# Masking and merging the live columns of the second query tile's two key tiles in a fused attention and expert kernel

## The reference

```python
xn = _layernorm(x)                       # (32, 256, 128)
Q, K, V = heads of xn @ Wq + bq, xn @ Wk, xn @ Wv
R = heads of xn @ Wr + br                # 10 position weights per head and row
d = jnp.arange(t)[:, None] - jnp.arange(t)[None, :]
valid = (d >= 0) & (d < maxlen)          # maxlen = 128
bias = jnp.where(valid, 0.0, NEG)
D_ntT = jnp.where(valid[None], b_nd[:, jnp.clip(d, 0, maxlen - 1)], 0.0)
extra = jnp.einsum('bhtn,ntp->bhtp', R, D_ntT)
logits = jnp.einsum('bhtd,bhpd->bhtp', Q, K) / math.sqrt(dq) + bias + extra
A = softmax(logits) @ V
out = x + (A joined) @ Wproj + bproj + experts(xn)
```

## Time and profile before

| | us |
|---|---|
| three timed runs | 1551.13, 1552.23, 1553.66 |
| median | 1552.23 |
| the profiled execution | 1553.0 |
| its span, first to last instruction | 1551.2 |
| TensorE busy | 1447.6 |
| VectorE busy | 1000.2 |
| ScalarE busy | 941.6 |
| GpSimd busy | 809.5 |
| transposes L1381, 1536 | 256.2 busy |
| copies L1073, 512 | 280.5 busy |
| sums L1093, 1024 | 304.7 busy |

### The profile page before, as it was taken

The page is one execution under the profiler, slowest core; times in us unless marked ns, Lnnn a source line. Parts: engine busy times, 40 slices in busy tenths (PEclk is TensorE's granted clock), DMA queues, the critical chain, the costliest instruction groups (busy, mean ns, idle before and its releaser), DMA issues.

```text
span 1551.2 us, 42996 instructions
## 1 busy us (share of the span) xinstructions
PE 1447.6 (93%) x11335; PEld 1157.8 (75%) x11335; DVE 1000.2 (64%) x3715; ACT 941.6 (61%) x2864; POOL 809.5 (52%) x1515
## 2 busy tenths in 40 slices
PE   2473999999999999999999999899999999999997
PEld 1132777777777777778999999677777777777776
DVE  4677777777777777772112211587778887877776
ACT  1130776767767676775455444477667677776765
POOL 0341777667776677671000000377766667777765
PEclk7695999999999999999999999899999999999999
DMA  9865765565666665545666665666665656666652
GB/s 284 279 237 178 211 184 163 169 176 171 180 174 181 170 177 170 166 138 170 207 200 202 203 211 181 175 180 174 180 177 169 176 164 180 175 181 177 176 166 66
DMA packets 375832, 283.10 MB, mean 183 GB/s; under 512 B 16635, under 2 KB 349989, under 8 KB 375717
## 3 DMA queue, kind: packets, MB, share of 16 engines
q1 hardware_dynamic: 367524, 265.16, 58.1%
q0 software_dynamic: 8192, 16.79, 3.4%
HBM read 168.57 MB, written 113.26 MB: 182 GB/s over the span
## 4 chain that ended last, share of the span: by engine, by line
PE 86%; SPq 5%; DVE 4%; issue 2%; ACT 1%; DMA 1%; POOL 0%; DVEq 0%; ACTq 0%; POOLq 0%
PE ps L1392 13%; PE ps L1412 12%; PE ps L1381 11%; PE ps L1281 9%; PE ps L1317 9%; PE ps L1282 9%; PE ps L1283 9%; PE ps L1422 9%; PE ps L1352 4%; SPq L435 1%; PE ps L1299 1%; SPq L396 1%; SPq L416 1%; DMA xn_d<-xn 1%; SPq L450 1%
## 5 line engine op out<-in xcount | busy, mean ns | idle before, releaser
L792 ACT ACTIVATE prob<-logit,low 128x128 f32<-128x128 f32 (+1 forms) x1024 | 454.4, 445 | 269.2 <-DVE low L1093 236.1
L1093 DVE CUSTOM_DVE_ANT_0 logit<-ps,extra 128x128 f32<-128x128 f32 (+1 forms) x1024 | 304.7, 353 | 155.9 <-issue 125.3
L1073 DVE COPY probT<-ps 128x384 f32<-128x384 f32 x512 | 280.5, 550 | 76.8 <-PE ps L1381 64.3
L666 POOL TENSOR_SCALAR prob<-prob,inv 128x128 f32<-128x128 f32 x512 | 190.5, 372 | 230.9 <-DVE inv L1083 220.4
L1381 PE MATMUL ps<-ident,prob 128*128 128x128 f32 x1536 | 256.2, 277 | 0.1
L668 POOL TENSOR_SCALAR prob<-prob,inv 128x256 f32<-128x256 f32 x512 | 243.2, 475 | 0.0
L1392 PE MATMUL ps<-qk 64*128 64x128 f32 (+1 forms) x2048 | 238.5, 351 | 0.7 <-DVE low L1093 0.7
L1381 PEld LDWEIGHTS ps<-ident,prob 128*128 128x128 f32 x1536 | 184.4, 141 | 40.2 <-issue 17.8
L1412 PE MATMUL ps<-probT,val 128*64 128x256 f32 (+1 forms) x2048 | 194.7, 332 | 4.3 <-DVE probT L1073 4.2
L641 POOL CAST r_hi<-r_raw 120x512 fp32r<-120x512 f32 x64 | 39.7, 620 | 297.3 <-ACT r_raw L763 297.2
L792 ACT ACTIVATION_READ_ACCUMULATOR prob<-logit,low 128x1 f32 x1024 | 191.7, 187 | 0.0
(11 more groups left out here) (171 smaller groups left out, 2544.6 us busy)
## 6 DMA issues: line engine op xcount, KB each, us to landing
skew<-gst SPq DMA_DIRECT2D x256, 256.0 KB
extra<-skew SPq DMA_DIRECT2D x128, 512.0 KB, 3.9
extra<-skew SPq DMA_DIRECT2D x128, 256.0 KB, 2.9
w1b<-w_d SPq DMA_DIRECT2D x39, 514.0 KB, 3.5
w2b<-w_d SPq DMA_DIRECT2D x39, 320.0 KB, 3.3
x_place<-zero SPq DMA_DIRECT2D x39, 256.0 KB, 2.8
placed<-x_place SPq DMA_DIRECT2D x39, 256.0 KB, 3.7
y_place<-yrow SPq DMA_DIRECT2D x39, 256.0 KB, 2.2
```

The costliest lines, as they stand in the source:

```text
L666: nc.gpsimd.tensor_scalar(prob[:, h, 0:P], prob[:, h, 0:P], inv[:, h, 0:1], 1.0, ALU.mult, ALU.mult).then_inc(norm_made, 1)
L792: ins = nc.scalar.activation(prob[:, h % PB, a:b], logit[:, h % LB, a:b], ACT.Exp, scale=-1.0, bias=low[:, h % LB, t:t + 1], accum_out=tot ...
L1073: nc.vector.tensor_copy(probT[:, h % 4, :], ps[:, PT_BANK[h % 2], 0:3 * P]).then_inc(pT_made, 1)
L1093: ins = nc.vector.tensor_tensor_reduce(out=logit[:, h % LB, a:b], in0=ps[:, S_BANK[n], a:b], in1=extra[:, h, a:b], scale=1.0, scalar=BIG, ...
```

## The change

The second query tile's logits are merged before the sums: a predicated copy on VectorE writes, for both heads at once, the logits of key tile 1 over those of key tile 0 where c <= p (`upto`). From there on a head has 2 x 128 columns instead of 3 x 128: `extra`, `logit`, `prob` shrink, the second sum, exponent and norm product have 128 columns, and two blocks are transposed. As the merged block holds weights for both key tiles, `copy_probs` writes it twice into `probT`, multiplied by 0/1 masks (`keep`), so that the value matmuls stay as they were. The position term has no fill in the second tile: each unit of it is written twice side by side (columns 0:128 and 128:256 of the scratch row) and the shifted read of 128 columns wraps round. The fill of the second tile's scratch falls away. The wide logits are issued before the narrow ones. GpSimd makes the masks at the beginning.

```diff
@@ memory
-        extra = sb("extra", [P, H, 3 * P])
+        extra = sb("extra", [P, H, 2 * P])
-        logit = sb("logit", [P, LB, 3 * P])
+        logit = sb("logit", [P, LB, 2 * P])
-        prob = sb("prob", [P, PB, 3 * P])
+        prob = sb("prob", [P, PB, 2 * P])
+        upto = sb("upto", [P, P])
+        keep = sb("keep", [P, 3 * P])
@@ SP
-            for tile in range(2):
-                sp.dma_start(skew_rows(tile, 0, H, P, P, ROW),
-                             fill[:, :].unsqueeze(1).broadcast_to([P, H, P])).then_inc(filled, 16)
+            sp.dma_start(skew_rows(0, 0, H, P, P, ROW),
+                         fill[:, :].unsqueeze(1).broadcast_to([P, H, P])).then_inc(filled, 16)
...
-                sp.dma_start(skew_rows(t, PER * g, PER, 0, P, ROW),
-                             gst[:, t, :].rearrange("p (h j) -> p h j", h=PER)
-                             ).then_inc(skew_out[t], 16)
+                src = gst[:, t, :].rearrange("p (h j) -> p h j", h=PER)
+                sp.dma_start(skew_rows(t, PER * g, PER, 0, P, ROW), src).then_inc(skew_out[t], 16)
+                if t == 1:
+                    sp.dma_start(skew_rows(t, PER * g, PER, P, P, ROW), src).then_inc(skew_out[t], 16)
...
-                wait_apart(sp, skew_out[t], (i * GROUPS + g + 1) * 16, filled)
+                wait_apart(sp, skew_out[t], (i * GROUPS + g + 1) * 16 * (t + 1), filled)
...
-                if t == 0:
-                    dst, src = extra[:, PER * g:PER * g + PER, 0:P], skew_rows(0, PER * g, PER, P - 1, P, ROW - 1)
-                else:
-                    dst, src = extra[:, PER * g:PER * g + PER, P:3 * P], skew_rows(1, PER * g, PER, -1, 2 * P, ROW - 1)
+                dst, src = extra[:, PER * g:PER * g + PER, t * P:(t + 1) * P], skew_rows(t, PER * g, PER, P - 1, P, ROW - 1)
@@ GpSimd: upto = 1 where c <= p; keep = 1 | p > c | c >= p
+            nc.gpsimd.memset(upto[:, :], 1.0).then_inc(mask_made, 1)
+            nc.gpsimd.memset(keep[:, :], 1.0).then_inc(mask_made, 1)
...
@@ ScalarE
-                        for t, (a, b) in enumerate(((0, P), (P, 3 * P))):
+                        for t, (a, b) in enumerate(((0, P), (P, 2 * P))):
@@ VectorE
-                wait_from(dve, skew_out[t], (seq * GROUPS + g) * 16)
+                wait_from(dve, skew_out[t], (seq * GROUPS + g) * 16 * (t + 1))
...
-                nc.vector.tensor_copy(probT[:, h % 4, :], ps[:, PT_BANK[h % 2], 0:3 * P]).then_inc(pT_made, 1)
+                nc.vector.tensor_tensor(probT[:, h % 4, 0:2 * P], ps[:, PT_BANK[h % 2], 0:2 * P], keep[:, 0:2 * P], ALU.mult)
+                nc.vector.tensor_tensor(probT[:, h % 4, 2 * P:], ps[:, PT_BANK[h % 2], P:2 * P], keep[:, 2 * P:],
+                                        ALU.mult).then_inc(pT_made, 1)
...
-                        for t, (a, b) in enumerate(((0, P), (P, 3 * P))):
+                        for t, (a, b) in enumerate(((0, P), (P, 2 * P))):
+                            if t == 1:
+                                nc.vector.copy_predicated(ps[:, 0:2, P:2 * P], upto[:, :].bitcast(U32).unsqueeze(1).broadcast_to([P, 2, P]),
+                                                          ps[:, 0:2, 2 * P:3 * P]).then_inc(logit_merged, 1)
+                                wait_apart(dve, logit_merged, i * PAIRS + j + 1, const_made)
@@ TensorE
-                for n in range(3):
+                for n in range(2):
                     mm = nc.tensor.transpose(ps[:, PT_BANK[h % 2], n * P:(n + 1) * P],
...
-                for q, k, cols in ((slice(0, P), slice(0, P), slice(0, P)), (slice(P, T), slice(0, T), slice(P, 3 * P))):
+                for q, k, cols in ((slice(P, T), slice(0, T), slice(P, 3 * P)), (slice(0, P), slice(0, P), slice(0, P))):
```

More of the change, by code:

```diff
@@ L211, in build @@
         assert top[0] <= yrow_at + 4 * 3 * P * 4
-        assert shared + (2 * ROW1 + 2 * ROW2 + ROWS_AHEAD * PER * E) * 4 <= shared + H * 3 * P * 4
+        assert shared + (2 * ROW1 + 2 * ROW2 + ROWS_AHEAD * PER * E) * 4 <= position_end
         top[0] = max(attention_end, prep_end)
@@ L298, in build @@
         s_psum = sem("s_psum")
+        logit_merged = sem("logit_merged")
         logit0_made = sem("logit0_made")
@@ L502, in spread_body @@
                 positions(i + 1, POSITIONS_AHEAD)
-            sp.wait_ge(filled, 32)
+            sp.wait_ge(filled, 16)
             for u in range(2):
@@ L607, in _ @@
             nc.gpsimd.memset(ones[:, :], 1.0).then_inc(const_made, 1)
+            nc.gpsimd.memset(upto[:, :], 1.0).then_inc(mask_made, 1)
+            nc.gpsimd.memset(keep[:, :], 1.0).then_inc(mask_made, 1)
+            pool.wait_ge(mask_made, 5)
+            nc.gpsimd.affine_select(out=upto[:, :], in_=upto[:, :], compare_op=ALU.is_ge, fill=0.0, base=0,
+                                    pattern=[[-1, P]], channel_multiplier=1).then_inc(mask_made, 1)
+            nc.gpsimd.affine_select(out=keep[:, P:2 * P], in_=keep[:, P:2 * P], compare_op=ALU.is_gt, fill=0.0, base=0,
+                                    pattern=[[-1, P]], channel_multiplier=1).then_inc(mask_made, 1)
+            nc.gpsimd.affine_select(out=keep[:, 2 * P:], in_=keep[:, 2 * P:], compare_op=ALU.is_ge, fill=0.0, base=0,
+                                    pattern=[[1, P]], channel_multiplier=-1).then_inc(mask_made, 1)
             pool.wait_ge(centred, 3)
@@ L1008, in _ @@
                 src, d = dst, 2 * d
-            upto = src
-            nc.vector.tensor_copy(tally[:, :], upto[:, TILES - 1, :]).then_inc(tally_made, 1)
+            upto_all = src
+            nc.vector.tensor_copy(tally[:, :], upto_all[:, TILES - 1, :]).then_inc(tally_made, 1)
             dve.wait_ge(counts_psum, 1)
@@ L1036, in _ @@
                                                 in1=counts[:, 0, :], op0=ALU.mult, op1=ALU.add))
-            link(nc.vector.tensor_tensor(upto[:, :, :], upto[:, :, :], chosen[:, :, :], ALU.subtract))
-            link(nc.vector.tensor_tensor(upto[:, :, :], upto[:, :, :], first[:, :].unsqueeze(1).broadcast_to(wide),
+            link(nc.vector.tensor_tensor(upto_all[:, :, :], upto_all[:, :, :], chosen[:, :, :], ALU.subtract))
+            link(nc.vector.tensor_tensor(upto_all[:, :, :], upto_all[:, :, :], first[:, :].unsqueeze(1).broadcast_to(wide),
                                          ALU.add))
             for k, one in enumerate((one1, one2)):
-                link(nc.vector.tensor_tensor(lg2[:, :, :], one[:, :, :], upto[:, :, :], ALU.mult))
+                link(nc.vector.tensor_tensor(lg2[:, :, :], one[:, :, :], upto_all[:, :, :], ALU.mult))
                 link(nc.vector.tensor_reduce(r1[:, :], lg2[:, :, :], AX_X, ALU.add))
@@ L1065, in weights @@
                                                in1=r_raw[:, k, :], op0=ALU.mult, op1=ALU.add).then_inc(r_made, 1)
-            dve.wait_ge(mask_made, 2)
+            dve.wait_ge(mask_made, 8)
             def copy_probs(i, h):
```

5 lines of the change are left out of this document (3 added, 2 removed).

## The result

The changed kernel takes 1545.3 us (median of six, 1542.8 to 1547.3), the kernel before 1552.3 beside it: a ratio of 0.9945, 95% interval 0.9934 to 0.9956. The forecast was 1524.4 us. The sign is right, and 7 us came where 28 were expected. The profiled execution took 1542.8 us, its span is 1541.0. Lines of the changed kernel: logits L1408 (before L1392), values L1428 (L1412), transposes L1397 (L1381), merge L1104, sums L1109 (L1093), masked products L1083 and L1084 (the copy L1073), `rT` L1074 (L1064), rounding on GpSimd L651, `low` and `logit` are written by the sums.

What follows compares the result with a forecast made beforehand. TensorE, busy 93% of the span, was taken as the bound, with VectorE next to be late. Terms -55.8 + 6.6 + 21.9 + 3 - 3.5 = -27.8 us took the median 1552.2 to 1524.4 us; range 1500 to 1562.

Steps and rivals of the forecast that it cites:

- Transposes, -55.8 us: TensorE: one of three transposes per head goes, 512 in all at 0.109 us; sequences 32.9 instead of 34.6 us.
- Order of the logits, 0: TensorE: issuing wide logits first is worth 0, bounds -0.05 to +0.05 us a pair.
- VectorE's prices: VectorE per pair: narrower sums -0.24, merge with wait +0.52, masked products +0.18; together +0.46 us.
- my case: Main forecast: merge row 0.42 us, partial stalls of TensorE, 1510 to 1535 us; chance 0.44.
- rival B: VectorE's merge reads two PSUM streams one after the other, row 0.69 us: 1544 us in all; chance 0.20.
- rival C: VectorE becomes the bound, merge passing source, old destination and mask singly, row over 0.9 us: 1565 us; chance 0.17.
- First half, slot 5 to 6, 0.41 us: TensorE waits for VectorE's second probability copy: 0.41 us per sequence, 16 x 0.41 = 6.6 us.
- the second half, slots 4 to 6, 1.37 us: TensorE stalls behind VectorE, 0.77 us at slot 4 and 0.6 at slot 6 per sequence: 21.9 us.
- Slot 4's mechanism: Second half: VectorE's expert-row additions plus the added work in slots 1 to 3 make slot 4's hand-over stall 0.77 us.
- the lag: Second half, slot 4: VectorE's copy starts 1.28 us after transposes, expected nearer the usual 0.58; slot 6 stall 0.6 us.
- Starts and preparation: Second position write adds 1.5 us at each of two attention starts, 3 us; one 1 MB fill less saves 3.5 us.
- Rival A: TensorE's stalls behind VectorE don't appear: -44 to -56 us, 1496 to 1508 us; chance 0.17.

Runs made afterwards that it cites:

- e1: The kernel before with two instead of three transposes per head, VectorE still copying 384 columns (third block's weights wrong): 1517.1 us, ratio 0.9770.
- f1 to f4: Changed kernel on one chip: wide logits first with VectorE's loops 1544.6 us, written out 1520.3; narrow first with loops 1544.4, written out 1521.6.
- g2: Changed kernel with VectorE's attention loops written out and GpSimd rounding position weights before the norm products of slots 1 and 4: 1506.2 us, ratio 0.9699.
- g3: g2 with ScalarE copying the unmasked block for both heads and VectorE making one masked product per head: 1505.1 us, ratio 0.9688.
- e3: Changed kernel with the predicated copy and its wait issued twice: 1626.2 us, ratio 1.0469.
- g1: Changed kernel with one sequence instead of two per turn of VectorE's loops: 1534.1 us, ratio 0.9869.

## Why the prediction was wrong

By its own steps:

- **Transposes, -55.8 us: right.** 32.90 us per sequence in e1, 32.9 forecast.
- **Order of the logits, 0: right** (f1 to f4).
- **VectorE's prices: right within 0.05 us.** The merge takes 0.57 instead of 0.52 us. Of this 0.11 is the value in a register, for which I had guessed 0.07 without a row. The masked products take 0.33 + 0.20 instead of 0.34 + 0.22. The merge's own row lasts 0.42 us, which is what the prediction named for my case, where rival B wanted 0.69 and rival C over 0.9; so both fall by their mechanism, and no run shows whether the old destination is read at all. That B's 1544 us is close to the time is a coincidence. The Trainium skill, VectorE: DVE Perf Modes, section The DRAIN you can't avoid, says that a semaphore after each Vector instruction costs nothing extra. The trace doesn't agree: the merge with its wait takes 0.46 us start to start at the least, where 0.34 was the distance without a wait. The Trainium skill, VectorE: DVE Perf Modes, section Why PSUM operands drop a tier, has one Vector read port for PSUM; no cost of it shows in the merge's row.
- **First half, slot 5 to 6, 0.41 us: right.** Slot 6 takes 4.27, which is 0.43 over 3.84, and even sequences take 33.33 us, 33.27 forecast.
- **The first step that failed: the first half was reckoned as 16 equal sequences.** The prediction put nothing for VectorE's loop. At six jumps VectorE loads its body anew and stands still, for 2.7 us in the rows above. In the kernel before, TensorE showed 0 to 0.9 us of it, 2.2 us at all six; after the change, with VectorE's slack used up, 1.5 to 1.9 each, 10.2 us in all. That is 8 us more than before, and in the second half it is another 2. No term, bound or rival held it.
- **The second step that failed: the second half, slots 4 to 6, 1.37 us.** Measured are 0.57 in slot 4, 0.10 in slot 5 and 1.04 in slot 6, together 1.71: plain sequences of 34.6 us, as long as before the change, where 34.2 was forecast. With the last sequence before the tail, in which VectorE waits 2.8 us for the rounding, this is 7 us in all. Slot 4's mechanism (row additions, then the merge) was right and smaller than the 0.77 forecast, so two errors of opposite sign hide one another in the sum. Slot 6's was wrong: I put the lag on a GpSimd instruction beside a copy and expected it to shrink, which the copy's start in slot 4 in fact did, to 0.47 us behind the transposes (1201.40 - 1200.93). In its place came a wait that I hadn't listed at all: VectorE's `rT` for GpSimd's rounding, 1.06 us, behind the row moves, which stand behind VectorE's own row additions. In the kernel before 0.01 us was to spare there, in the sequence whose rows stand under e1.
- **Starts and preparation: right as far as the runs can tell.** First logits at 150.0 instead of 152.1 us (-2 forecast). But they scatter by more than 1 us either way between runs (150.7 to 153.2 us in the runs built on the changed kernel, 152.4 to 153.9 in those on the kernel before); from VectorE's first `rT` to the first logits the second start got 1.0 us longer (1.5 forecast).
- Rival A's time (no stalls, 1496 to 1508) is reached once both faults are mended, by g2's 1506.2 and g3's 1505.1 us; the kernel of the prediction never had it.

Added up for the two profiled executions, 1553.0 and 1542.8 us: 10.2 us came where 27.8 were forecast, so 17.6 are missing. The jumps are 10 of them, slots 4 to 6 of the second half 7. What is left is small and of both signs. The largest piece is the first sequence of the first half, which got 0.2 us longer instead of 1.3 shorter; in it too VectorE waits for the rounding, 2.0 us.

## What to carry to other kernels

When a change spends an engine's slack, list all the idle time that this engine has per period, also that with no releaser and that which the bounding engine doesn't yet show: loop jumps, and waits on a third engine. Each becomes a term, with the slack that is left as its cover. A loop body is best kept small enough that no instruction packets appear in the DMA view, or written out, and a helper's small operation goes ahead of its long ones where another engine waits for it. And variants are compared with the changed kernel run beside them on the same chip: the kernel before, with slack, is no control for one without.

## What the hardware showed

- VectorE's body of two sequences has five to six instruction packets in two sequences and, at the jumps shown, 1.7 us (before), 1.55 + 1.13 us (after) or 2.68 + 2.85 us (e3, seven packets) of idle time; one of half the size has no packets and no idle time from loading (g1).
- A predicated copy of 128 x 256 from PSUM into PSUM runs 0.42 us, as long as a sum of that width with one PSUM operand.
- With a wait of VectorE for its own last instruction, 0.42 us long, it is 0.46 us from start to start if the value is a constant, and 0.57 if it is in a register and one more wait stands in front.
- The same kernel took 1544 us on one chip and 1565 on another, on which the kernel before took 1554 on both, with TensorE's signal in one slot of eight 0.02 or 0.68 us behind its last matmul. The cause is open, and so is whether it is the chip's.
